# Attention on one core: value products placed in pairs of key blocks

## The reference

```python
for i in range(H):
    att = jnp.einsum('btd,bsd->bts', q_rot, k_rot) * scale
    if cascade_bias is not None:
        att = att + cascade_w[i - 1] * cascade_bias
    att = jnp.where(causal, -jnp.inf, att)
    att = jax.nn.softmax(att, axis=-1)
    out_i = jnp.einsum('bts,bsd->btd', att, v[:, i])
    head_outputs.append(out_i)
    cascade_bias = jnp.mean(att, axis=1, keepdims=True)
```

## Time and profile before

| | |
|---|---|
| time, median of 3 runs | 3421.09 us (3419.45 to 3431.74) |
| span of the profiled execution | 3421.5 us |
| PE busy | 3079.1 us (90%) |
| ACT busy | 3055.5 us (89%) |
| DVE busy | 2747.6 us (80%) |
| POOL busy | 2127.2 us (62%) |
| mean granted TensorE clock | 0.967 of 2.4 GHz |

### The profile page before, as it was taken

The page is one execution under the profiler, slowest core; times in us unless marked ns, Lnnn a source line. Parts: engine busy times, 40 slices in busy tenths (PEclk is TensorE's granted clock), DMA queues, the critical chain, the costliest instruction groups (busy, mean ns, idle before and its releaser), DMA issues.

```text
span 3421.5 us, 95130 instructions
## 1 busy us (share of the span) xinstructions
PE 3079.1 (90%) x29668; PEld 1592.4 (47%) x29668; DVE 2747.6 (80%) x9925; ACT 3055.5 (89%) x8882; POOL 2127.2 (62%) x6194
## 2 busy tenths in 40 slices
PE   7898888888999899999999989999999988989855
PEld 3444444443544445554554434555455544544544
DVE  7777777777888788888988897888888987888754
ACT  4999999999989989999999998999999999989634
POOL 6556566564655467876666666777766645666245
PEclk8999999999999999999999999999999999999976
DMA  5322223223334324444433423444334433444354
GB/s 164 94 79 87 85 59 87 76 73 90 93 101 111 104 84 120 120 123 131 128 111 112 123 64 110 116 120 145 104 111 117 125 83 100 130 118 136 97 185 126
DMA packets 270810, 371.12 MB, mean 108 GB/s; under 512 B 61669, under 2 KB 177389, under 8 KB 270304
## 3 DMA queue, kind: packets, MB, share of 16 engines
q1 hardware_dynamic: 255056, 326.65, 33.2%
q0 software_dynamic: 14976, 37.34, 3.8%
q10 hardware_dynamic: 272, 1.05, 0.1%
HBM read 260.02 MB, written 104.40 MB: 107 GB/s over the span
## 4 chain that ended last, share of the span: by engine, by line
PE 36%; DVE 8%; issue 7%; ACT 5%; POOL 4%; SPq 2%; DMA 1%; another core or an unknown queue 1%; POOLq 0%; DVEq 0%; ACTq 0%
PE pv L1240 8%; PE scores L1209 7%; PE scores L1222 6%; DVE att_a L1527 4%; PE side L1369 3%; PE side L1269 2%; ACT att_t L1406 2%; ACT att_a L1396 2%; PE side L1295 2%; PE side L1376 1%; PE scores L1224 1%; PE side L1283 1%; PE scores L1369 1%; SPq L2028 1%
## 5 line engine op out<-in xcount | busy, mean ns | idle before, releaser
L1396 ACT ACTIVATE att_a<-att_a,neg_max 128x128 f32<-128x128 f32 (+7 forms) x2048 | 1609.8, 786 | 52.5 <-DVE neg_max L1527 48.7
L1406 ACT ACTIVATE att_t<-scores 128x1024 f32<-128x1024 f32 (+7 forms) x2048 | 1343.0, 656 | 68.7 <-PE scores L1224 53.7
L1527 DVE CUSTOM_DVE_ANT_0 att_a<-scores,window 128x512 f32<-128x512 f32 (+3 forms) x2048 | 1146.8, 585 | 240.2 <-PE scores L1209 133.7
L1209 PE MATMUL scores<-k_stack,q_stack 99*128 99x512 bf16 (+3 forms) x3072 | 919.0, 335 | 132.6 <-DVE neg_max L1527 112.1
L1240 PE MATMUL pv<-att_t,v_sb 128*32 128x256 f32 (+7 forms) x16384 | 898.8, 299 | 1.9 <-ACT att_t L1406 1.7
L1222 PE MATMUL scores<-q_stack,k_stack 104*128 104x512 bf16 (+3 forms) x3072 | 842.7, 332 | 62.8 <-ACT att_t L1406 50.2
L1527 DVE CUSTOM_DVE_ANT_0 att_a<-scores,window,neg_max 128x512 f32<-128x512 f32 (+3 forms) x1024 | 557.8, 545 | 110.4 <-PE scores L1209 92.9
L1209 PEld LDWEIGHTS scores<-k_stack,q_stack 99*128 99x128 bf16 x3072 | 280.1, 98 | 572.8 <-DVE neg_max L1527 345.6
L1240 PEld LDWEIGHTS pv<-att_t,v_sb 128*32 128x32 f32 x16384 | 340.0, 108 | 413.0 <-issue 334.1
L1222 PEld LDWEIGHTS scores<-q_stack,k_stack 104*128 104x128 bf16 x3072 | 275.3, 98 | 402.4 <-issue 197.9
L1224 PE MATMUL scores<-identb,mask 128*128 128x128 bf16 x2048 | 451.9, 222 | 0.0
(11 more groups left out here) (307 smaller groups left out, 4367.5 us busy)
## 6 DMA issues: line engine op xcount, KB each, us to landing
runner_r<-in_experts SPq DMA_DIRECT2D x137, 384.0 KB
qk_parts<-of_proj SPq DMA_DIRECT2D x128, 384.0 KB
of_proj<-in_xt SPq DMA_DIRECT2D x29, 1024.0 KB
q_stack<-qk_parts SPq DMA_DIRECT2D x256, 96.0 KB
k_stack<-qk_parts SPq DMA_DIRECT2D x256, 96.0 KB
q_stack<-qk_parts SPq DMA_DIRECT2D x256, 64.0 KB
k_stack<-qk_parts SPq DMA_DIRECT2D x256, 64.0 KB
head_out<-o_sb SPq DMA_DIRECT2D x252, 64.0 KB
```

What stands on the lines that cost most here:

```text
L1209: engine.matmul(piece_room(c), qs[0:ROWS_A, i * P:(i + 1) * P], ks[0:ROWS_A, low:high], start=True, stop=True).then_inc(s_a_filled, 1)
L1396: engine.activation(taken, taken, EXP, scale=-1.0, bias=neg_max[:, n, i:i + 1], accum_out=row_sum[:, n, i:i + 1]).then_inc(s_exp_a, 1)
L1406: engine.activation(att_t[:, ring:ring + end - base], scores[:, base:end], EXP, accum_out=col_sum[:, n, j:j + 1]).then_inc(s_exp_b, 1)
L1527: engine.tensor_tensor_reduce(out=att_a[:, ring + low:ring + high], in0=piece_room(c), in1=window[:, T - A_LONG[p] + low:T - A_LONG[p] + h ...
```

## The change

A value product is placed for two key blocks at once. The timetable has one `pv` stage for each pair (0 and 1, 2 and 3, ...), with the key of the second; it needs the exponential of the second block, and costs the columns of both and one fixed 0.2 us where there were two. What waits for one block in the timetable now waits for its pair; the copy of `pv` to `o_sb` is due ahead of the next unit's first pair. In the program of PE the stage calls `att_v` for both blocks, one behind the other. The instructions, their number and their semaphore counts stay.

```diff
             if kind == "pv":
-                busy = cols_b(key[1]) * 0.42e-3 + 0.2
+                busy = (cols_b(key[1] - 1) + cols_b(key[1])) * 0.42e-3 + 0.2
                 return busy, busy + 0.07
...
+        def pair_of(k):
+            return divmod(k | 1, TB)
...
-            "PE": [[("fill_a", k) for k in pieces], [("fill_b", k) for k in blocks], [("pv", k) for k in blocks],
+            "PE": [[("fill_a", k) for k in pieces], [("fill_b", k) for k in blocks],
+                   [("pv", (u, p)) for u, p in blocks if p % 2],
                    [("rows", x_) for x_ in range(1, UNITS + 1)]],
...
                 yield "exp_b", key
-                if p == 0:
+                if p == 1:
                     if u:
                         yield "o_move", u - 1
...
                 if block(*key) >= NET:
-                    yield "pv", of_block(block(*key) - NET)
+                    yield "pv", pair_of(block(*key) - NET)
...
             elif kind == "pv":
-                k = block(*key) + NET
+                k = block(*key) - 1 + NET
                 t = start_of(("exp_b", of_block(k))) - HANDOVER if k < BLOCKS else start_of(main[-1]) + 10
             elif kind == "o_move":
-                t = due("pv", (key + 1, 0)) - 0.7 if key + 1 < UNITS else start_of(main[-1]) + 10
+                t = due("pv", (key + 1, 1)) - 0.9 if key + 1 < UNITS else start_of(main[-1]) + 10
...
                     elif kind == "pv":
-                        att_v(*n)
+                        u, p = n
+                        att_v(u, p - 1)
+                        att_v(u, p)
```

## The result

| | kernel before | changed kernel |
|---|---|---|
| time, median | 3425.23 us (3419.45 to 3431.74, 4 runs) | 3458.68 us (3450.73 to 3461.53, 4 runs) |
| profiled execution: span | 3421.5 us | 3448.9 us |
| last value product begins | 3208.9 us | 3241.8 us |

What follows compares the result with a forecast made beforehand. ACT's work was taken as the floor, with PE most often late for it in the second stage. An 82 us gain less 12 us left 70: 3421.5 - 70 = 3351.5, called 3352 us, range 3298 to 3410.

Steps and rivals of the forecast that it cites:

- The price of a run: PE's value products: merging two runs into one saves 0.25 us, 849 fewer runs giving 212 us of PE time.
- The rival in which the second block's loads cost 0.21 us inside the pair: Within the hidden-relief rival (chance 0.18): only 0.04 us saved per merger on PE, giving 13 us, 3408 us.
- 0.83 x 0.51 x 194 = 82 us: Second stage: 0.83 us of PE relief per unit, 0.51 us of ACT idle for each, over 194 units.
- half lies on the chain: 81 us: Second stage: of 161 us of PE time freed, half lies on the chain that ended last, gaining 81 us.
- From the 82 I take 12 us for DVE's share and denser side work: Second stage: deduction of 12 us, from between 0 and 41, leaving a gain of 70 us.
- The estimate by two stages: First against second stage: ACT idle rises 0.61 us a unit, PE 1.19, so 0.51 per us of PE; 82 us.
- The rival on the slow side: Second stage: thin PE stretches lower the granted clock to a mean near 0.89; 3440 to 3470 us, chance 0.09.
- First block: Each pair's first value product waits some 1.5 us longer for the second's exponential; costed at nothing, 100 us if cover went.
- length: A pair holds PE 0.72 us uncut, against 0.68 for the largest single block; 0.04 us more, costed at nothing.
- copy: The copy of `pv` gets more room; at best 9 us of PE time comes back, left out of the sum.
- last part: After the last value product: taken as unchanged at 212 us.
- The first stage: 100 to 800 us: ACT is at its floor, so 51 us of PE relief hides behind it; gain 0.

Runs made afterwards that it cites:

- e4: The changed kernel with the timetable's cost of a pair at the columns plus 0.3 us instead of 0.2: 3327.7 us, ratio 0.992 to the kernel before.
- e2: The kernel before with the timetable's cost of a single block at the columns plus 0.1 us instead of 0.2: 3452.28 us, ratio 1.030.
- e5: The changed kernel itself, measured on a chip of the experiments: 3369.64 us, ratio 1.0037 to the kernel before.
- e8: The changed kernel with every side stage on PE costed 15% higher in the timetable: 3305.79 us, ratio 0.984 to the kernel before.
- e12: The changed kernel with side stages on DVE, not on PE, costed 15% higher in the timetable: 3316.16 us, ratio 0.989 to the kernel before.
- e6: The kernel before, unchanged, run once for its trace on a chip of the experiments: 3360.48 us.
- e9: Control: the changed kernel with the timetable's handover time at 0.045 us instead of 0.035: 3365.97 us, ratio 1.0037 to the kernel before.
- e10: Control: the kernel before, single blocks, with the timetable's handover time at 0.045 us instead of 0.035: 3341.73 us, ratio 0.996.
- e3: The kernel before with its timetable unchanged, but PE does both blocks of a pair at the second block's place: 3391.0 us, ratio 1.0115.
- e13: The changed kernel's order, with first blocks of each unit's second and third pair multiplied earlier, 1,535 runs instead of 1,023: 3447.89 us, ratio 1.028.
- e7: The kernel before with the timetable's cost of a single block at the columns plus 0.25 us instead of 0.2: 3405.02 us, ratio 1.014.

## Why the prediction was wrong

**The price of a run: right, a little high.** The forecast took 0.25 us from single rows. Over the trace of the kernel before, at full granted clock, the median of a block of 256 columns a group is 0.57 us to the next matmul and that of one of 32 is 0.20, together 0.77. The three other sums of two blocks come to 0.77 as well, and a pair takes 0.63. With the 0.09 us ahead of a run a merger saves 0.23 us, 849 of them 195 us of PE time instead of 212. The rival in which the second block's loads cost 0.21 us inside the pair is out.

**The step that failed** is what the freed time of PE is worth. It was wrong in both of its terms.

The first is the main one: "0.83 x 0.51 x 194 = 82 us", and by the chain "half lies on the chain: 81 us". With the side work about where it was (e4), the pairs gave 0.8%, 27 us, a third of that. The chain of the changed kernel shows what was left out: once PE is earlier, ACT and DVE take its place on the chain, so a share of one half holds for the first microseconds and not for 161. That this is why 27 us came and not 82 is argued from the chain; no run shows it by itself.

The second is the deduction: "From the 82 I take 12 us for DVE's share and denser side work". (The prediction calls that "nearer the upper value" of 0 to 41; 12 is nearer to 0.) From e4 to the change, with pairs in both, the timetable's cost goes from 0.3 to 0.2 us a pair and the ratio from 0.992 to 1.0037: about 39 us. I had seen the density in the order (projections in 18 transposes instead of 26) and costed it as if a queue that is laid closer still finds its time. On the chips of the experiments this makes 27 - 39 = -12 us where +70 was forecast. It is a way from the kernel before to the change by way of e4, and not a check of the change by other runs.

**Both terms depend on each other.** The corners, by ratio:

| | side work placed about as before | as in the change |
|---|---|---|
| single blocks | 1 | 1.030 (e2) |
| pairs | 0.992 (e4) | 1.0037 (e5) |

Pairs are worth 0.8% in the first column and 1.030 - 1.0037 = 2.6% (88 us) in the second, and 2.9% (98 us) with 15% on PE's side stages. Denser side work costs 1.2% with pairs and 3.0% with single blocks. So the relief of PE is worth most where the plan asks most of PE, and the forecast of 82 us is met only in a layout that is slower for it. e8 bounds this account: with side work nearly as dense by units as in the change it is 1.6% faster than the kernel before. So the place by units does not by itself say what a layout costs.

**The estimate by two stages** (0.51 us of ACT idle for each us of PE) compared a stage without finishing and tiles with one that has both. The kernel before ran 194 units there with 0.82 us of ACT idle each, with every side stage placed where, by the timetable's costs, nothing becomes late. I read that idle time as PE's load. The better reading, which e8 and e12 support and no run shows directly, is that it is in good part the difference between plan and execution: the change lowers the load and fills it up again, so the plan's reserve stays as small as before, while DVE, ACT and POOL get their side stages closer together.

**The clock.** The rival on the slow side was priced at a mean clock of 0.89. It was 0.97 against 0.98, by my 0.2 us for each us at half clock about (0.01 x 2400/0.5) x 0.2 = 10 us. On the chip of e5 and e6 the clock is 0.99 and 0.98, and the change is slower there as well; it is a companion at most.

**First block, length, copy, last part: right.** ACT waited 0.7 us for value products, and the last part is 5.5 us shorter, not longer.

**The first stage: right, as far as can be told.** Costed at 0, it gave one unit in 60 on the first chip and on that of e5 and e6. With the order changed in detail it is the other way round: 60 units for the pairs (e9) and 61 for the single blocks (e10), so no gain is shown.

**Left open.** On the first chip the loss is 0.9%, on the others 0.4%, and the kernel before itself is 2% slower there; the trace shows 28 us of that behind the last value product (212.6 against 185.0 us), and nothing was tried on the cause. Also open is why pairs in the old order (e3) lose 1.2% while taking pairs apart at the change's order (e13) loses 2.4%; both fit the view that an order serves the runs it was planned for, and neither says which wait carries it. The edits of costs move density, detail and the accuracy of the plan together. The controls bound only the detail, at 0.4% or 13 us, which is the uncertainty of the 27 and of the 39 us as well.

## What to carry to other kernels

When a planner lays out work by costs, a cheaper operation is not slack: ask what the planner will put into the time, and measure that apart, by giving the new operation a cost that leaves the rest where it was (e4) and the old operation the new cost (e2). And price a relief by the engine that comes next on the chain, not by the share of the chain that it has before. Let a plan keep room on purpose; here 15% on the side stages of PE turned a loss of 0.4% into a gain of 1.6%. And look at both ends of such a knob: too sparse (e7) shortens the attention by 66 us and lengthens the end by 109.

## What was not expected of the hardware

A run of column-group matmuls costs its two changes of mode once, for one block or two (the drain of the Trainium skill's "TensorEngine Tiling (Array Packing)", Key Properties, agrees; the page gives no price): two blocks, 288 columns a group in all, take 0.63 us where they take 0.77 us apart, and in the changed kernel 757 unnamed waits of the weight loads are left of 1353. By the loads' busy time the opposite could be read: they rose from 340.0 us in the kernel before to 430.5 us in the change at the same count of 16384,

```profile
L1244 PEld LDWEIGHTS pv<-att_t,v_sb 128*32 128x32 f32 x16384 | 430.5, 110 | 311.1 <-issue 184.8
```

while the pairs became shorter; a busy sum of overlapping loads says little of time. And the same program differs by 2% from one chip to another, more than most of the differences of this study (e2 and e13 apart), which is why each ratio stands against runs of the kernel before on its own chip.
